# A small clear on GpSimd behind each row scatter and behind the first 27 of 39 output scatters

## The reference

```python
x = x + gnn0(layernorm(x), adj)   # tanh filter of adj*adj, top 350 of a row, two products, relu
x = x + ffn0(layernorm(x))        # 8 experts, top 2 by gate, hidden 256
x = x + gnn1(layernorm(x), adj)   # (A + I) scaled by degree, product with w, elu
x = x + ffn1(layernorm(x))        # causal attention, 4 heads, then 8 experts, top 2, hidden 341

# the last step of ffn1, which is the part that the change touches
probs = softmax(flat @ router_w.T)
tp, ti = top_k(probs, 2); tp = tp / (sum(tp) + 1e-9)
for e in range(8):
    hh = silu(flat @ w1[e].T) * (flat @ w3[e].T)
    out = out + weights[:, e:e+1] * (hh @ w2[e].T)
```

## Time and profile before

| | |
|---|---|
| median of 3 timed runs | 577.62 us (574.78 to 579.01) |
| span of the profiled execution | 610.4 us |
| that execution's own device time | not given; the span alone is |
| busy share PE, DVE, ACT, POOL | 82%, 70%, 51%, 42% |
| mean TensorE clock granted | 0.913 of full |
| indirect transfers by POOL | 32 to `slots_in`, 39 to `slots_out` |

### The profile page before, as it was taken

The page is one execution under the profiler, slowest core; times in us unless marked ns, Lnnn a source line. Parts: engine busy times, 40 slices in busy tenths (PEclk is TensorE's granted clock), DMA queues, the critical chain, the costliest instruction groups (busy, mean ns, idle before and its releaser), DMA issues.

```text
span 610.4 us, 11302 instructions
## 1 busy us (share of the span) xinstructions
PE 501.5 (82%) x3819; PEld 281.4 (46%) x3819; DVE 429.3 (70%) x1065; ACT 314.3 (51%) x522; POOL 254.2 (42%) x275
## 2 busy tenths in 40 slices
PE   2999986699999799996776888998969657498880
PEld 1533334477777445443322432333412157397770
DVE  6898838888999925757786896999752038166564
ACT  0787985869999001201254453764745334166661
POOL 3000005133436401102364895997353632555562
PEclk9999995999999799999578789999989859599996
DMA  8999954100139250110233522003035447389925
GB/s 302 409 421 422 405 189 149 42 19 20 34 129 411 85 109 0 39 26 15 68 110 99 157 72 60 2 1 104 35 129 177 176 121 222 112 277 384 324 89 175
DMA packets 39570, 93.43 MB, mean 153 GB/s; under 512 B 7488, under 2 KB 24944, under 8 KB 35168
## 3 DMA queue, kind: packets, MB, share of 16 engines
q1 hardware_dynamic: 35072, 86.96, 40.6%
q0 software_dynamic: 2272, 4.69, 2.2%
q10 hardware_dynamic: 2176, 1.13, 0.6%
HBM read 69.39 MB, written 21.00 MB: 148 GB/s over the span
## 4 chain that ended last, share of the span: by engine, by line
PE 54%; DVE 21%; ACT 7%; issue 6%; another core or an unknown queue 5%; DMA 4%; POOL 1%; SPq 1%; DVEq 0%; POOLq 0%; ACTq 0%
PE ps L1578 8%; DVE A L2385 7%; PE ps L1755 6%; PE ps L1489 6%; PE ps L1506 6%; PE ps L1404 5%; PE ps L1859 3%; PE ps L1656 3%; PE ps L1747 3%; DMA R<-in_adj_in 3%; PE ps L1842 2%; PE ps L1603 2%; PE ps L1381 1%; DVE bst L1916 1%
## 5 line engine op out<-in xcount | busy, mean ns | idle before, releaser
L2385 DVE TENSOR_REDUCE A<-ps 128x1 f32<-128x512 f32 (+3 forms) x160 | 86.3, 601 | 13.7 <-PE ps L1656 13.0
L1302 ACT ACTIVATE A<-ps 128x1024 f32<-128x1024 f32 (+3 forms) x80 | 68.4, 894 | 49.2 <-PE ps L1747 40.3
L1007 POOL TENSOR_TENSOR G<-G,A 128x1024 f32<-128x1024 f32 (+3 forms) x40 | 73.8, 1888 | 9.1 <-ACT A L1302 8.9
L1656 PE MATMUL ps<-A 96*128 96x512 f16 (+3 forms) x160 | 55.4, 388 | 10.4 <-DVE A L2385 5.1
L1578 PE MATMUL ps<-A,G 128*128 128x512 f32 x128 | 62.1, 611 | 0.0
L1404 PE MATMUL ps<-R,G 128*128 128x512 f32 x128 | 59.2, 605 | 1.0 <-DVE G L1959 0.8
L1859 PE MATMUL ps<-A 128*128 128x128 f16 (+1 forms) x702 | 50.3, 228 | 6.0 <-issue 6.0
L1506 PE MATMUL ps<-R 128*128 128x128 f16 x768 | 48.2, 219 | 6.7 <-DVE x L2077 5.8
L1506 PEld LDWEIGHTS ps<-R 128*128 128x128 f16 x768 | 45.3, 98 | 14.3 <-issue 6.6
L1747 PE MATMUL ps<-A 97*128 97x512 f16 (+3 forms) x160 | 45.2, 366 | 6.9 <-ACT A L1302 5.1
L2059 DVE SCALAR_TENSOR_TENSOR R<-R 128x512 f16<-128x512 f32 x64 | 46.7, 754 | 5.0 <-ACT R L1157 4.7
(11 more groups left out here) (311 smaller groups left out, 933.0 us busy)
## 6 DMA issues: line engine op xcount, KB each, us to landing
A<-w_split SPq DMA_DIRECT2D x39, 533.0 KB
A<-in_adj_t SPq DMA_DIRECT2D x16, 1024.0 KB, 17.5
slots_in<-xn SPq DMA_DIRECT2D x1, 8320.0 KB, 22.4
R<-in_adj_in SPq DMA_DIRECT2D x7, 1024.0 KB, 6.1
w_split<-A SPq DMA_DIRECT2D x9, 725.0 KB, 4.1
xn<-in_adj_in SPq DMA_DIRECT2D x5, 1024.0 KB
xT<-in_adj_in SPq DMA_DIRECT2D x4, 1024.0 KB
A<-in_f_w SPq DMA_DIRECT2D x16, 170.5 KB
```

The lines of the kernel that those rows point to most:

```text
L1007: pool.tensor_tensor(total, total, probabilities(n, pair)[:, :, t0:CW], ALU.add).then_inc(s_sum, 1)
L1302: act.activation(probabilities(n, pair)[:, :, t0:CW], ps[:, 2 * pair:2 * pair + 2, t0:CW], ACT.Exp, scale=1.0 / (SQ * SQ * float(HD) ** 0. ...
L1656: last = pe.matmul(ps[:, bank, 0:width], queries(t // TPC, h)[0:KQ, P * (t % TPC):P * (t % TPC) + P], keys(b, h // (NH // NKV))[0:KQ, 0:wi ...
L2385: dve.reduce_max(pm[:, h, t % TPC, b:b + 1], ps[:, bank, 0:width], AX_X).then_inc(s_rmf, 1)
```

## The change

Behind every `scatter_rows`, and behind `scatter_output(n)` for n below 27, POOL now clears the first 256 columns of the buffer `xT` (128 partitions, fp32), which nothing reads any more by then. Each clear but the first waits on a semaphore until the clear before it has finished. This makes 32 + 27 = 59 clears. A semaphore that nothing used gives up its place for the new one. Nothing is removed, and no other engine's program changes.

```diff
@@ names
+        unused = xT[:, 0:CW // 2]
...
-        s_hhi = sem("hidden0_high")
+        s_pause = sem("pause_over")
...
+        SPACED = 27
@@ gpsimd
+            paused = iter(range(2 * NT + SPACED))
+
+            def pause():
+                n = next(paused)
+                if n:
+                    pool.wait_ge(s_pause, n)
+                pool.memset(unused, 0.0).then_inc(s_pause, 1)
+
@@ scatter_group
                         scatter_rows(g, t, which)
+                        pause()
@@ gpsimd, group 2 and the outputs
             for t in range(GTS[2]):
                 for which in range(2):
                     scatter_rows(2, t, which)
+                    pause()
             for n in range(SLOTS):
                 scatter_output(n)
+                if n < SPACED:
+                    pause()
```

## The result

The changed kernel takes 583.04 us, median of 4 runs (579.73 to 584.68), against 577.1 us for the kernel before in the same comparison (574.78 to 579.01): a ratio of 1.0105, interval 1.007 to 1.0141. The forecast was 570 us and faster. The change makes the kernel slower by about 1%, and the first rival named 583 to 601 us for that.

A forecast was written before the change was run, and what follows sets the result against it. The prediction took stalls beside POOL's scatter runs, 32.7 us, as the cost to cure; the profiled execution would gain 18.4 us, and with 0.6 of the stalls in timed runs -7.6 us from 577.62 gave 570 us, range 556 to 588 us.

The forecast's parts named there:

- the first rival: Stalls are in the recorded execution alone and the clears lengthen POOL: 583 to 601 us, likeliest 586, chance 0.30.
- The chain of waits and the link to runs of scatters: Some 30 us of unknown waits, in attention and slot phases, belong to runs of POOL's scatters, not to missing data.
- From the profile to the timed runs: Carries -18.4 us on the recorded span of 610.4 us to -7.6 us on the timed median of 577.62 us.
- the share f: Part of the recorded stalls that timed runs have; taken as 0.6, change worth 8.7 - 27.1 f us, even at 0.32.
- the stalls' 32.7 us: Total stall time in the recorded execution: 15.1 us ahead of the slot phase and 17.6 us in it.
- the prediction's own sum: Without stalls in timed runs, the kernel before ends its last scatter at 574.7 us, the changed one at 583.4: +8.7 us.
- What a clear costs: On POOL, each clear between scatters adds 0.33 us, between bounds of 0.03 and 0.63 us.
- Group 1 gates slot 0: Group 1's 16 scatters take 25.8 us and become what slot 0 waits for; slot 0 is transposed at 490.6 us.
- POOL runs the outputs back to back: From group 2 on POOL runs without a pause: 27 outputs with clears take 45.9 us, 12 without take 16.4 us.
- that it alone sets the end: POOL is the last to end, its output scatters finishing at 583.4 us in the profiled execution.
- the even case: Gains and costs cancel, or clears do not end a run of scatters: 572 to 583 us, likeliest 578, chance 0.28.
- The Trainium skill's rule: By it there is nothing to cure; the prediction said the trace disagrees for the recorded execution.

The follow-up runs named there:

- the second record: The kernel before, unchanged, timed and recorded again: 576.7 us against 577.54 us, ratio 0.9974, recorded span 576.2 us.

## Why the prediction was wrong

**The chain of waits and the link to runs of scatters.** In the execution shown, the unknown time did lie beside scatters, and its excess of 34 us lies behind 436 us. But that was a property of this one execution. Two more records are without it, and no timed run is long enough to hold it. That scatters cause the stalls is not shown.

**"From the profile to the timed runs" is the step that failed.** It set the share f of the stalls in timed runs at 0.6; the runs put it at about 0. The gap of 32.8 us and the stalls' 32.7 us were nearly equal, and the rival said so. I held against it that it left nothing for the clock, and gave up to 20.3 us of the gap to the low clock in the earlier trace rows. A low clock in one execution is a difference from others only if they lack it: the second record has 0.96 and 0.79 in the same windows. With f = 0 the prediction's own sum gives +8.7 us; measured is +5.9.

**What a clear costs.** I took 0.33 us between bounds of 0.03 and 0.63. It is 0.20: the clear takes 0.33, but the gap ahead of the next scatter shrinks by 0.13. The reading that the gap belongs wholly to the scatter was half right.

The price alone doesn't close the sum. It holds 51 clears, so 0.20 for 0.33 takes off 51 x 0.13 = 6.6 us and leaves +2.1, less than the +5.9 measured. One more error is known. For f = 0 the sum kept the 22.0 us of group 1 in the recorded execution, with 1.7 us of pauses between its scatters; the second record takes 20.3 us (458.75 to 479.03). That gives +3.8; what remains to +5.9 (4.0 to 8.1) is not resolved. That the prediction's +8.7 comes near the measured time is in part luck.

**Group 1 gates slot 0: right.** The chain to slot 0 goes over the load of these rows in every record but the one of the earlier trace rows, where the stalled attention ended last. Group 1's clears alone cost 2.7 us (1.4 to 4.0), and 3.0 us in the trace. The group 0 clears cost nothing, as forecast, though for another reason than the one given: POOL waits for DVE's positions behind them.

**POOL runs the outputs back to back: right; that it alone sets the end: wrong.** In the second record of the kernel before POOL still had 3.0 us of waits for ACT, and longer gaps; in the changed kernel it has 0.5 us. First the kernel before, then the changed one (columns as in the earlier trace rows):

```profile
POOL slots_out L1059 <- issue: 13.1, 35, 0.6
POOL slots_out L1059 <- ACT A L1350: 3.0, 4, 1.2
```

```profile
POOL slots_out L1069 <- issue: 7.5, 37, 0.3
POOL slots_out L1069 <- ACT A L1364: 0.5, 2, 0.3
```

But followed back from the end, the chain leaves POOL at 564.25 us for ACT, PE and the weight load. It holds no clear of group 2 and none behind an output. The prediction had POOL as the only limit from group 2 on. Output clears alone measured +1.0 us (-0.2 to 2.5). From slot 0 to the last output scatter the changed kernel takes 83.06 us and the second record of the one before 80.93. Single records don't settle this difference: with clears behind rows alone it is 83.31 us.

The 24.5 us in the earlier trace rows, on which the even case leant, belonged to the rare execution.

**The Trainium skill's rule** (SBUF — State Buffer, "Who interferes with whom"), by which a DMA never contends with a compute engine and PE and ACT never wait on anyone, is not contradicted by any ordinary record here: without the stalls there is nothing for it to explain. The prediction said that the trace disagrees with it for the recorded execution; that goes too far, since the rule is about the ports of SBUF and no row shows what PE waited for. What held PE up in the one record of the earlier trace rows stays open. It came with scatters and didn't come again in the 12 further records, so whether clears would end it was never tested. Nor is it known which chip that record came from; the experiments ran on two chips.

**The range** of 556 to 588 us held 583.04, because its upper end stood for this rival. The chances (0.42 faster, 0.30 slower) leaned the wrong way because they rest on f.

## What to carry to other kernels

Before reading a stall, set the span of the recorded execution against the timed runs: a span well above the median is of another execution than the ones that are timed, and its unexplained waits are the first suspects for the difference. Explain the gap only with what is known to differ between executions, not with what merely looks slow in the one at hand. And an engine with a small share of the chain can still gate: here POOL held 2% of it, and 3 us more on one run of its scatters came out as 2.7 us (1.4 to 4.0) at the end.

## What the runs showed of the hardware

- A clear of 128x256 fp32 between two indirect transfers added 0.20 us start to start (1.485 against 1.287), one of 128x1 nothing (1.28), and two of 128x256 of which the second waits for the first 0.84 us (2.12). The gap ahead of the next transfer was 0.30 us without a clear, 0.17 us behind one of 128x256 and 0.45 us behind two.
- Device time lay 1.7 to 2.1 us above the span in every execution that has both (577.93 with 576.2, 579.73 with 577.7).
- In one execution DVE, ACT and PE were held up beside runs of scatters, for 4 to 9 us at a time. The scatters themselves took 0.98 us there, as ever. What brings that about was not found.
